# The inter product with 128-column weights, and the state product in two halves

## What is computed

```python
q = heads(x @ Wq.T + bq); k = heads(x @ Wk.T + bk); v = heads(x @ Wv.T + bv)
q = softmax(exp(beta) * q, axis=-1)      # over the 8 features of a head
k = softmax(exp(beta) * k, axis=-1)
kv = cumsum(einsum('zsD,zsd->zsDd', k, v), axis=1)   # running state, causal
kn = cumsum(k, axis=1)
num = einsum('zsD,zsDd->zsd', q, kv)
den = sum(q * kn, axis=-1, keepdims=True)
out = (num / den) @ Wo.T + bo
```

## Time and profile before

| | |
|---|---|
| median of 3 runs | 1406.88 us |
| profiled execution's own time | 1401.46 us |
| its span, first to last instruction | 1399.4 us |
| mean granted TensorE clock | 0.971 of full |
| TensorE matmul busy | 1236.7 us (88%) |
| weight loads busy | 712.4 us (51%) |
| VectorE busy | 1024.8 us (73%) |
| ScalarE busy | 579.1 us (41%) |
| GpSimd busy | 322.2 us (23%) |

### The profile page before, as it was taken

One profiled execution on the slowest core, in us unless ns is written; L12 is line 12 of the kernel. 1 busy time (PEld: TensorE's weight loads), 2 busy tenths in 40 slices (PEclk: granted clock), 3 DMA queues, 4 the chain that ended last, 5 costly groups with the idle time before them and its releaser, 6 DMA issues.

```text
span 1399.4 us, 81215 instructions
## 1 busy us (share of the span) xinstructions
PE 1236.7 (88%) x36322; PEld 712.4 (51%) x36322; DVE 1024.8 (73%) x2031; ACT 579.1 (41%) x1049; POOL 322.2 (23%) x590
## 2 busy tenths in 40 slices
PE   1569999989999999999989999999999989999996
PEld 1335455545555555555555555555555555555553
DVE  3757678777778677877777787777678777777772
ACT  1534344344344344444434444444344344444431
POOL 3122222222222122222222222222222222222210
PEclk8789999999999999999999999999999999999998
DMA  9022323243233233323323332333233233223321
GB/s 222 6 65 60 76 77 74 75 81 73 75 79 72 65 84 80 71 75 77 71 75 84 74 76 75 84 71 79 73 81 71 73 84 75 76 75 84 60 60 41
DMA packets 181141, 105.99 MB, mean 76 GB/s; under 512 B 120160, under 2 KB 153056, under 8 KB 180832
## 3 DMA queue, kind: packets, MB, share of 16 engines
q1 hardware_dynamic: 180112, 99.79, 29.8%
q10 hardware_dynamic: 720, 1.31, 0.3%
HBM read 40.20 MB, written 16.78 MB: 41 GB/s over the span
## 4 chain that ended last, share of the span: by engine, by line
PE 86%; issue 9%; DVE 2%; DMA 1%; POOL 0%; ACT 0%; SPq 0%; POOLq 0%; DVEq 0%; ACTq 0%
PE s_ps L887 10%; PE a_ps L979 7%; PE a_ps L960 6%; PE a_ps L998 6%; PE vo_ps L860 5%; PE vo_ps L942 5%; PE k_ps L860 5%; PE vo_ps L871 4%; PE vo_ps L862 4%; PE vo_ps L864 4%; PE k_ps L864 4%; PE k_ps L862 4%; PE vo_ps L875 4%; PE vo_ps L873 4%; PE q_ps L864 4%
## 5 line engine op out<-in xcount | busy, mean ns | idle before, releaser
L507 ACT ACTIVATE q_heads<-qT,cst 128x512 f32<-128x512 f32 x256 | 164.0, 711 | 88.2 <-DVE qT L752 88.2
L400 POOL TENSOR_TENSOR y_sum<-y,y_magic 128x512 f32<-128x512 f32 x64 | 81.4, 1272 | 429.3 <-DVE y_magic L614 429.3
L660 DVE TENSOR_TENSOR att<-s_ps,cst 128x512 f32<-128x512 f32 x256 | 163.8, 681 | 3.3 <-PE s_ps L887 3.3
L393 POOL TENSOR_TENSOR x_split<-xn,x_split 128x512 f16<-128x512 f32 x64 | 74.2, 1160 | 397.9 <-ACT x_split L455 391.1
L887 PE MATMUL s_ps<-q_heads,kT 32*32 32x128 f32 x8192 | 148.9, 273 | 2.5 <-issue 1.6
L498 ACT ACTIVATE q_e<-q_shift,q_exp_scale 128x512 f32<-128x512 f32 x64 | 46.2, 722 | 250.0 <-DVE q_shift L632 250.0
L887 PEld LDWEIGHTS s_ps<-q_heads,kT 32*32 32x32 f32 x8192 | 114.1, 104 | 56.3 <-issue 56.2
L979 PE MATMUL a_ps<-st_seqs,q_heads 128*32 128x36 f32 x8192 | 98.8, 201 | 46.2 <-issue 44.4
L713 DVE TENSOR_TENSOR vp<-vo_ps,vp 128x512 f32<-128x512 f32 x64 | 44.3, 692 | 121.0 <-PE vo_ps L864 121.0
L979 PEld LDWEIGHTS a_ps<-st_seqs,q_heads 128*32 128x32 f32 x8192 | 87.2, 109 | 79.1 <-issue 77.2
L860 PE MATMUL k_ps<-w_hi,xT 128*128 128x512 f16 x256 | 99.1, 387 | 18.3 <-DMA xT<-x_split 11.4
(11 more groups left out here) (136 smaller groups left out, 2456.0 us busy)
## 6 DMA issues: line engine op xcount, KB each, us to landing
v_groups<-vp SPq DMA_DIRECT2D x1024, 18.0 KB, 2.4
x_in<-L_attn_x SPq DMA_DIRECT2D x64, 256.0 KB
x_res<-L_attn_x SPq DMA_DIRECT2D x64, 256.0 KB
out<-o_sb SPq DMA_DIRECT2D x64, 256.0 KB
w_own<-L_attn_Wk SPq DMA_DIRECT2D x1, 1024.0 KB, 12.6
w_own<-L_attn_Wq SPq DMA_DIRECT2D x1, 1024.0 KB, 14.7
w_own<-L_attn_Wv SPq DMA_DIRECT2D x1, 1024.0 KB, 16.3
att<-L_ffn_weight_fp SPq DMA_DIRECT2D x1, 1024.0 KB, 17.9
```

Of the source, the lines that this page charges most:

```text
L393: gp.tensor_tensor(x_split[:, 1, :], xn[:, :], x_split[:, 0, :], ALU.subtract)\
L400: gp.tensor_tensor(y_sum[:, :], y[:, :], y_magic[:, :], ALU.add).then_inc(ysum_ready, 1)
L507: last = sc.activation(q_heads[:, i.parity, :, j, :], qT[:, :, :], ACT.Copy, scale=head_mask[:, j:j + 1])
L660: v.tensor_tensor(att[:, c, :, :, :].rearrange("p g j s -> p (g j) s"), s_ps[:, DM * (c % 2):DM * (c % 2 + 1)].rearrange("p (h s) -> p h s ...
```

## The change

The inter product becomes 16 matmuls, one for each group, whose weights are the queries of the group's four heads side by side (128 columns) and whose output is all 128 partitions; the 36 columns that move are the same. The state product is cut in two halves of 32 matmuls (8 groups each); the first half follows the first half of the scores and the second the second, if step i exists. The semaphores `state_done` and `masked_ready` count two for a step. On VectorE `mask_state` is cut likewise: its first half follows the first two masks of the scores, ahead of `al`; its second half stays where both were.

```diff
--- before.py
+++ after.py
@@ -474,7 +474,7 @@
                 if i.exists():
                     act.wait_ge(kshift_ready, (i + 1).n)
                     if i.after(2):
-                        act.wait_ge(state_done, (i - 1).n)
+                        act.wait_ge(state_done, (i - 1).n * 2)
                         act.wait_ge(kT_ready, (i - 1).n)
                     sc.activation(k_e[:, i.parity, :], k_shift[:, :], ACT.Exp, scale=k_exp_scale[:, :])\
                         .then_inc(ke_ready, 1)
@@ -632,20 +632,19 @@
                 v.tensor_tensor(heads(sh[:, :]), heads(bank[:, :]), per_head(mx[:, :]), ALU.subtract)\
                     .then_inc(sh_ready, 1)
 
-            def mask_state(t):
-
-                dve.wait_ge(state_done, (t + 1).n)
-                for n in range(2):
-                    half = slice(n * G // 2, (n + 1) * G // 2)
-                    last = v.tensor_tensor(
-                        st_masked[:, half, :, :],
-                        a_state[:, n, :].rearrange("p (g j w) -> p g j w", j=J, w=VW),
-                        head_mask[:, None, :, None].to_broadcast([P, G // 2, J, VW]), ALU.mult)
-                last.then_inc(masked_ready, 1)
+            def mask_state(t, n):
+
+                dve.wait_ge(state_done, t.n * 2 + n + 1)
+                half = slice(n * G // 2, (n + 1) * G // 2)
+                v.tensor_tensor(
+                    st_masked[:, half, :, :],
+                    a_state[:, n, :].rearrange("p (g j w) -> p g j w", j=J, w=VW),
+                    head_mask[:, None, :, None].to_broadcast([P, G // 2, J, VW]), ALU.mult)\
+                    .then_inc(masked_ready, 1)
 
             def add_state(t):
 
-                dve.wait_ge(masked_ready, (t + 1).n)
+                dve.wait_ge(masked_ready, (t + 1).n * 2)
                 v.tensor_reduce(st_step[:, :, :], st_masked[:, :, :, :].rearrange("p g j w -> p g w j"),
                                 AX.X, ALU.add).then_inc(ststep_ready, 1)
                 dve.wait_ge(ststep_ready, (t + 1).n)
@@ -688,7 +687,7 @@
                     .then_inc(ksum_ready, 1)
                 dve.wait_ge(ksum_ready, (i + 1).n)
                 if i.after(2):
-                    dve.wait_ge(state_done, (i - 1).n)
+                    dve.wait_ge(state_done, (i - 1).n * 2)
                     for b in range(SEQS):
                         dve.wait_ge(v_moved[i.parity][b], i.half * 16 * GL)
                 v.reciprocal(vp[:, i.parity, :, DH].rearrange("p (l q j) -> p q l j", l=GL, j=J),
@@ -727,6 +726,8 @@
                 if t.exists():
                     mask_scores(t, 0)
                     mask_scores(t, 1)
+                    if i.exists():
+                        mask_state(t, 0)
                 if (i - 2).exists():
                     dve.wait_ge(ah_ready, (i - 1).n)
                     v.tensor_tensor(flat(al[:, :, :]), t_ps[:, :], flat(ah[:, :, :]), ALU.subtract)\
@@ -751,7 +752,7 @@
                         dve.wait_ge(qheads_ready, i.n)
                     v.transpose(qT[:, :, :].rearrange("p g s -> p (g s)"), q_e[:, :]).then_inc(qT_ready, 1)
                 if t.exists() and i.exists():
-                    mask_state(t)
+                    mask_state(t, 1)
                 if fold:
                     dve.wait_ge(bvo_done, 1)
                     v.scalar_tensor_tensor(bias[:, 3, :], vo_ps[:, :], out_dn[:, :], bias[:, 3, :],
@@ -889,6 +890,22 @@
                                       q_heads[rows, t.parity, GL * gq + gl, :, :], start=True, stop=True)
                 last.then_inc(scores_done, 1)
 
+            def state(t, n):
+
+                if n == 0:
+                    pe.wait_ge(ke_ready, (t + 1).n)
+                    pe.wait_ge(vp_ready, (t + 1).n)
+                    if t.after(1):
+                        pe.wait_ge(an_ready, t.n)
+                    pe.sem_inc(pe_waited, 1)
+                for g in range(n * G // 2, (n + 1) * G // 2):
+                    col = DM * n + J * VW * (g % (G // 2))
+                    for b in range(SEQS):
+                        rows = slice(TOK * b, TOK * (b + 1))
+                        last = mm(a_ps[rows, col:col + J * VW], k_e[rows, t.parity, TOK * g:TOK * (g + 1)],
+                                  vp[rows, t.parity, v_head(g):v_head(g) + J, :], start=True, stop=True)
+                last.then_inc(state_done, 1)
+
             def body(i, low_part=True, last_weights=None, fold=False):
                 if i.exists():
                     pe.wait_ge(x_turned, (i + 1).n * 16)
@@ -901,6 +918,8 @@
                     if t.after(1):
                         pe.wait_ge(att_ready, t.n * 4)
                     scores(t, 0)
+                    if i.exists():
+                        state(t, 0)
                 t = i - 2
                 if t.exists():
                     pe.wait_ge(an_ready, (t + 1).n)
@@ -928,6 +947,8 @@
                 if t.exists():
                     pe.wait_ge(att_ready, t.n * 4 + 2)
                     scores(t, 1)
+                    if i.exists():
+                        state(t, 1)
                 if fold:
                     pe.wait_ge(vp_ready, 1)
                     pe.wait_ge(wl_ready, chunks)
@@ -945,21 +966,6 @@
                             last = mm(vo_ps[:, :], xq[:, t.slot, c, :], w_lo[:, MF, c, :], start=False,
                                       stop=False, skip_group_check=True)
                     last.then_inc(f_done, 1)
-                t = i - 1
-                if t.exists() and i.exists():
-
-                    pe.wait_ge(ke_ready, (t + 1).n)
-                    pe.wait_ge(vp_ready, (t + 1).n)
-                    if t.after(1):
-                        pe.wait_ge(an_ready, t.n)
-                    pe.sem_inc(pe_waited, 1)
-                    for g in range(G):
-                        col = DM * (g // (G // 2)) + J * VW * (g % (G // 2))
-                        for b in range(SEQS):
-                            rows = slice(TOK * b, TOK * (b + 1))
-                            last = mm(a_ps[rows, col:col + J * VW], k_e[rows, t.parity, TOK * g:TOK * (g + 1)],
-                                      vp[rows, t.parity, v_head(g):v_head(g) + J, :], start=True, stop=True)
-                    last.then_inc(state_done, 1)
                 t = i - 2
                 if t.exists():
                     pe.wait_ge(ah_ready, (t + 1).n)
@@ -969,16 +975,16 @@
                 if t.exists():
                     pe.wait_ge(qheads_ready, (t + 1).n)
                     if i.exists():
-                        pe.wait_ge(masked_ready, (t + 1).n)
+                        pe.wait_ge(masked_ready, (t + 1).n * 2)
                     else:
                         pe.wait_ge(an_ready, t.n)
                     if t.after(1):
                         pe.wait_ge(stseqs_ready, t.n)
                     for g in range(G):
-                        for j in range(J):
-                            mm(a_ps[TOK * j:TOK * (j + 1), a_col(g):a_col(g) + GW],
-                               q_heads[:, t.parity, g, j, :], st_seqs[:, t.parity, g, :, :],
-                               start=(g % (G // 2) == 0), stop=False, skip_group_check=True)
+                        mm(a_ps[:, a_col(g):a_col(g) + GW],
+                           q_heads[:, t.parity, g, :, :].rearrange("p j s -> p (j s)"),
+                           st_seqs[:, t.parity, g, :, :],
+                           start=(g % (G // 2) == 0), stop=False, skip_group_check=True)
                 if i.exists():
                     if fold:
                         pe.wait_ge(fold_ready, 1)
```

## The result

The changed kernel takes 1424.03 us (median of 4 runs, 1423.49 to 1426.22) beside 1406.52 us for the kernel before: the ratio is 1.0147, 95% interval 1.0108 to 1.0186. It is slower by 1.5%; I had forecast 1353 us, 3.8% faster. The profiled span is 1421.9 us, against 1399.4.

A forecast was written before the change was run, and what follows sets the result against it. TensorE's own step plus stalls for instruction blocks of 256 was taken as the bound; +13 us for the longer step and -67 us of stalls gave -54, from 1406.88 to 1353 us, range 1322 to 1400.

The forecast's parts named there:

- the price of a pair of the inter product: TensorE's inter product: each load and matmul pair takes 0.058 us, 32 pairs 1.86 us, +0.50 us a step.
- the rival that went with it: Inter product: a full-width f32 weight load is slower, up to 0.12 us a pair, 3.84 us, 1478 us in all; chance 0.10.
- Its own threshold, 0.085: Inter product: us a pair from which the slower weight load decides and the forecast is wrong.
- the row at 0.058: Profile row of f32 transposes on TensorE: second load starts 0.06 us behind the first, taken as 0.058 a pair.
- the bound at 0.12: Inter product: upper bound of a pair, the cost of a whole transpose with 128 moving columns, 3.84 us in all.
- The stalls: TensorE waiting for instruction blocks of 256: fewer short blocks, 0.33 a step for 0.86, gain 67 us of 108.
- the 30 to 50 us of "issue": PE's waits: "issue" idle expected to remain after the change, with hardly any at L979.
- The start of the inter product: TensorE reaches it 12.87 us after the K projection, before 13.17, without waiting for VectorE's mask, 0.09 to spare.
- the rival in which VectorE decides: First mask does not fit ahead of `al`; inter product starts at 13.17, +19 us, 1372 us in all; chance 0.14.

The follow-up runs named there:

- e4: The changed kernel with each inter matmul moving 18 columns instead of 36; four executions of 1472.69, 1488.5, 1518.29 and 1540.53 us.
- e6: The changed kernel with each inter matmul moving 72 columns instead of 36; 1414.51 us, ratio to the kernel before 1.0038.
- e7: The kernel before with the state product whole, directly behind the second half of the scores, ahead of the fp8 product; 1414.48 us, ratio 1.0052.
- e1: The changed kernel (state product in halves) with the old inter product of 64 matmuls of 32 weight columns; 1385.25 us, ratio to before 0.9829.
- e5: The kernel before with the inter product in 32 matmuls of 64 weight columns, state product whole in its old place; 1361.32 us, ratio 0.9681.
- e3: The changed kernel with the inter product in 32 matmuls of 64 weight columns; 1331.07 us, ratio to before 0.9447.
- e2: The kernel before with the new inter product of 16 matmuls of 128 weight columns, state product whole in its old place; 1484.03 us, ratio 1.0509.

## Why the prediction was wrong

**The step that failed is the price of a pair of the inter product.** I took 0.058 us, from the second load of the transposes, and multiplied by 32 to 1.86 us. It is 0.111, 3.56 us in all: 1.70 x 63 = 107 us more than forecast, which is more than the whole miss of 71. The mechanism was right (the load paces the product, e4 and e6), the size was not, and the row was of another kind: a transpose's load of the same form takes 141 ns, a product's 193. It was the nearest row by form and not by kind. I had also read only the first two of the four loads; the kernel before shows all four in 0.42 us:

```profile
704.30 0.42 PEld L912 LDWEIGHTS t_ps<-cst,a_n 128*128 128x128 f32 x4 [0.20 <-issue]
```

Two took 0.20, so the third and the fourth come 0.11 us apart, and not 0.06. Whether the load or the 128 moving columns sets that distance these rows don't tell, but they don't show a sequence of pairs at 0.058 anywhere. The two windows that showed the second load 0.06 behind the first show this for the product's (timeline of the changed kernel, weight loads):

```profile
718.22 0.19 PEld L984 LDWEIGHTS a_ps<-st_seqs,q_heads 128*128 128x128 f32 x1 [0.57 <-issue]
...
718.22 0.30 PEld L984 LDWEIGHTS a_ps<-st_seqs,q_heads 128*128 128x128 f32 x2 [0.57 <-issue]
```

The second load begins 0.11 us behind the first. The page that I weighed against the row, TensorE: Matmul & The Clock Gate, LDWEIGHTS, of the Trainium skill, gives 107 ns for 128 columns; for the product the trace agrees with it (0.111 a pair, 0.875 ns a column), for the transpose it doesn't. I gave the rival that went with it 0.10. It was the right mechanism at somewhat too high a price, 0.12 a pair. Its own threshold, 0.085, was the place to hesitate: the row at 0.058 and the bound at 0.12 stood on both sides of it, and only a guess said to which kind of load the product belongs.

**The stalls were right in cause and too small in gain.** Forecast -67 us, measured -83 in the waits, -91 with the correction. The distance of 256 instructions, the packets (forecast 240, measured 241) and the effect of the longest run (the waits of e7 against e1) hold; the 30 to 50 us of "issue" that I expected to be left are 13.0. The page Runtime: NRT & Kernel Launch, Instruction fetch mechanics, of the Trainium skill, calls the fetch hidden; with 96 us of it before, these runs disagree. But I gave the gain to the count of instructions and the runs together. e1 shows that the even runs alone, with the inter product at 256 instructions, save 16 us in waits, and e5 that 128 instructions fewer save 57.5.

**The start of the inter product was right, for other reasons.** It is 12.94 us against 12.87 forecast. But TensorE was free at 12.67, 0.2 earlier than I had it, since the shape no longer changes behind the fp8 product (0.88 us, forecast 0.97) and behind the output projection (2.59, forecast 2.70); VectorE's mask, forecast for 12.68, ended at 12.84. So the rival in which VectorE decides came true in small: 0.27 us in this step, some 16 us over the 54 steps in which the mask releases the product, hidden in the total because TensorE came earlier. The halves are worth 24, 30 and 60 us beside an inter product of 32, 64 and 128 columns (before to e1, e5 to e3, e2 to the changed kernel).

**The clock was missing from the sum.** It changed little between the two kernels, 4 us, but from 28 us in e6 to 85 in e4 among the experiments, and it is 31 of the 60 us between e2 and the changed kernel.

## What to carry to other kernels

Take the price of a weight load from a product of the same kind, not from a transpose of the same form; where one row and one bound lie on both sides of the point at which the change stops paying, the chance is not 0.1. Fewer, wider matmuls trade loads side by side on strips for loads in a row: count load columns on the fullest strip, beside the instructions saved, and try the width between. Idle of TensorE with no releaser, at even distances in instructions, is code that has not come; long runs of small matmuls want to be broken up by long ones.

## What was not expected of the hardware

With the same instructions, 18 instead of 36 moving columns in 32 of some 470 matmul records of a step made the kernel slower, 1473 and 1489 us in the two shortest executions against 1424, and 72 made it faster, 1415; the pairs stayed as far apart. All of it lay in the granted clock (means 0.942, 0.974, 0.980). Which property of the work the clock follows, the columns or the values, was not tried further. A f32 product's loads took 0.875 ns a column on one strip and went side by side on several; a transpose's took 141 ns where the product's took 193. TensorE's stalls over 1 us lay at multiples of 256 of its instructions, and nearly all ended 1.2 to 1.6 us after a packet of code had come.
